# Self-attention in a decoder layer: the transposes of the probabilities stand ahead of the product of probabilities and values in each slot on TensorE

## The chip, the cores and the metric

The kernel runs on one core of one Trainium2 chip, as one program and one launch. The metric is device time in microseconds (us), the median of the runs of a kernel. The engines are named as the profile names them: PE (TensorE, the matrix engine) with PEld for its weight loads, DVE (VectorE), ACT (ScalarE), POOL (GpSimd) and SP (SyncE, which issues most transfers).

## The reference, cut to what matters

One decoder layer: self-attention, cross-attention to a second sequence and a mixture of 16 experts with a shared feed-forward part, each followed by a residual and a layer norm. The change lies in the self-attention, on 32 sequences of 256 tokens with 256 channels, 16 heads and one latent of 72 that serves as keys and as values of every head:

```python
Wdkv = x @ latent_w + latent_b                                  # keys and values, 72 wide
q = jnp.einsum('btc,hcl->bhtl', x, Wd_w) + Wd_b[None, :, None, :]
scores = jnp.einsum('bhtl,bsl->bhts', q, Wdkv) / sqrt(d_head)
scores = jnp.where(causal[None, None, :, :], scores, -jnp.inf)
attn = jax.nn.softmax(scores, axis=-1)
y = jnp.einsum('bhts,bsl->bhtl', attn, Wdkv)
z = jnp.transpose(y, (0, 2, 1, 3)).reshape(b, t, h * Wdkv.shape[-1])
return z @ out_w + out_b
```

## The kernel before

**Numbers in two parts.** Nearly every product is made from operands that are split into a high and a low part (`_hi`, `_lo`). ACT copies a result out of its PSUM bank as the high part; DVE subtracts that from the bank and writes the low part. A bank is free for its next product only when DVE has read it. `three` (lines 128 to 132) then issues three matmuls for one product, `two` (lines 135 to 139) two.

**Slots.** Self-attention is a software pipeline of slots, one for each pair of heads of a sequence, so 256 in all (in the code `g`), and every engine walks through the same list of slots `m` with its own part of the work. In slot m, PE works on five different pairs at once, each at another stage (`SL, IL, TL, PL, OL = 6, 7, 8, 10, 12`): the scores of pair m-6, the transposes of the probabilities of pair m-8, the product of probabilities and values of pair m-10, and the output projection of pair m-12. The probabilities are a triangle of three 128x128 blocks for a head, so a slot has six transposes, three for each of the pair's two heads (`hh`).

**Groups.** 16 slots are a group: two sequences. In the first slot of a group PE projects the latent of the group's two sequences (`KV_MM`), and in the second it transposes that (`KV_TR`) into the keys' and values' other layout. A group has nine tiles of queries to project, in the slots that `Q_SLOT` lists (2, 3, 5, 6, 8, 9, 11, 12, 14). So slots 1, 4, 7, 10, 13 and 15 of a group have no projection on PE; they are called bare slots below. The output projection isn't even either: it has 8 matmuls in most slots, but where four pairs share filled-up rows (`packed`) it has 4, 4, 10 and 10. In the order of PE, the 4s come in slots 0, 1, 8 and 9 of a group, the 10s in slots 2, 3, 10 and 11.

**Banks.** PE has one bank `Q` for projections, two banks `SC` for scores, two banks `TR` for transposes (one for each `hh`), one bank `PV` for the product of probabilities and values, and two banks `O`. In a slot DVE reads the score banks (line 922), makes the reciprocals of the sums (934), writes the low part of the projection if there is one (945), the low part of y from bank `PV` (957) and the two low parts of the transposed probabilities from the banks `TR` (964). ACT copies out the projection (833), then y (844), then the two transposed heads (852), and takes the four exponentials (865). POOL scales the probabilities by the reciprocals (599, 601), a slot ahead of the transposes. Each engine does its instructions strictly in this order.

**What PE waits for.** Before the transposes of head `hh` PE waits for POOL's scaled probabilities (`p_done`) and for DVE to have read the same bank in the slot before (`pTlo_done` of pair g-1). Before the product of probabilities and values it waits for the low parts of its operand, made two slots earlier (`pTlo_done` of pair g), and for DVE to have read bank `PV` in the slot before (`ylo_done` of g-1). ACT waits for that product (`pv_mm`) before it copies y, and y stands ahead of the two transposed heads on ACT and on DVE.

After slot 264 the cross-attention begins; it and the experts follow and are not touched.

Of the kernel before, what the change touches and what calls it, by code (L numbers as in the profile page):

```python
# [33 lines left out]
P = 128  # L34
# [11 lines left out]
RING = 4  # L46
# [17 lines left out]
def need(eng, sem, count):  # L64

    if not isinstance(count, int) or count > 0:
        if isinstance(sem, Later):
            eng.wait_ge(sem.own, sem.base + count)
        else:
            eng.wait_ge(sem, count)  # L70
# [57 lines left out]
def three(pe, out, stat_hi, stat_lo, mov_hi, mov_lo, start, stop):  # L128

    pe.matmul(out, stat_hi, mov_hi, start=start, stop=False, skip_group_check=True)  # L130
    pe.matmul(out, stat_hi, mov_lo, start=False, stop=False, skip_group_check=True)  # L131
    return pe.matmul(out, stat_lo, mov_hi, start=False, stop=stop, skip_group_check=True)  # L132


def two(pe, out, stat_hi, stat_lo, mov_hi, mov_lo, start, stop):

    pe.matmul(out, stat_hi, mov_hi, start=start, stop=False, skip_group_check=True)  # L137
    rows = slice(0, AT + REST)
    return pe.matmul(out, stat_lo[rows], mov_lo[rows], start=False, stop=stop, skip_group_check=True)  # L139
# [48 lines left out]
def upto_slot(J, g, per=1, more=0):  # L188

    return J * (SA_BODY * per) + (per * (g + 1) + more)  # L190


def upto_group(J, c, per=1, more=0):

    return J * (SA_GROUPS * per) + (per * (c + 1) + more)
# [7 lines left out]
def upto_tile(J, t, per=1, more=0):  # L203

    return J * (SA_GROUPS * QT * per) + (per * (t + 1) + more)
# [17 lines left out]
def slot_exists(J, g):  # L223
    return not isinstance(J, int) or 0 <= SA_BODY * J + g < B * NP


def group_exists(J, c):
    return not isinstance(J, int) or 0 <= SA_GROUPS * J + c < GROUPS
# [59 lines left out]
def self_attention(nc, al, bank, ident, cross, d):  # L288
# [28 lines left out]
    prob = al.sb("prob", [P, RING, 2, 3 * P])  # L317
# [9 lines left out]
    Q, SC, TR, PV, O = bank[0], bank[1:3], bank[3:5], bank[5], bank[6:8]  # L327
# [3 lines left out]
    def first_body(J):  # L331
        return isinstance(J, int) and J == 0
# [10 lines left out]
    def kv_bank(J, c):  # L343

        return PV if isinstance(J, int) and SA_GROUPS * J + c == 0 else Q
# [18 lines left out]
    inv_done, p_done = al.sem("inv_done"), al.sem("p_done")  # L364
    p_tr, pThi_done, pTlo_done = al.sem("p_tr"), al.sem("pThi_done"), al.sem("pTlo_done")
# [22 lines left out]
    SL, IL, TL, PL, OL = 6, 7, 8, 10, 12  # L388
# [254 lines left out]
    def tensor(pe):  # L643
# [33 lines left out]
        def slot(J, m):  # L677
            g = m - SL
            if slot_exists(J, g):
                c, p, i = g // GROUP, g % GROUP // 2, g % 2  # L680
                r, k = p % RING, c % 2
# [9 lines left out]
                for hh in range(2):  # L691
                    need(pe, s_read, upto_slot(J, g - 1, 4, 2 * hh - 2))
                    for t in range(TT):
                        tk, keys = slice(t * P, t * P + P), slice(0, (t + 1) * P)
                        mm = two(pe, SC[hh][:, t * T:t * T + (t + 1) * P], q[:, r, hh, 0, i, tk], q[:, r, hh, 1, i, tk],
                                 kvT_a[:, k, i, keys], kvT_b[:, k, i, keys], True, True)
# [4 lines left out]
            elif u == KV_MM and group_exists(J, c):  # L701
                need(pe, xlo_done, upto_row(J, c, 1))
                need(pe, qlo_done, upto_tile(J, c * QT - 1))
                for k in range(KC):
                    mm = three(pe, kv_bank(J, c)[:], lw_hi[:, k], lw_lo[:, k], x_hi[:, c, k], x_lo[:, c, k], k == 0, k == KC - 1)
# [6 lines left out]
            if t is not None and group_exists(J, c):  # L712
                j = t % QT
                w = slice(j * P, j * P + P)
                if first_body(J) and t in SPLIT_BEFORE:
                    pe.wait_ge(w_lo, SPLIT_BEFORE[t])
                if j == 0 and kv_bank(J, c) is Q:
                    need(pe, kv_done, upto_group(J, c))
                elif first_body(J) and t == DIRECT // 2:
                    pe.wait_ge(head_lo, 1)  # L720
                else:
                    need(pe, qlo_done, upto_tile(J, t - 1))
                for k in range(KC):
                    mm = three(pe, Q[:], wd_hi[:, k, w], wd_lo[:, k, w], x_hi[:, c, k], x_lo[:, c, k], k == 0, k == KC - 1)
                mm.then_inc(q_mm, 1)
            g = m - PL
            if slot_exists(J, g):
                r, k, i = g % 2, g // GROUP % 2, g % 2
                if g % GROUP == 0:
# [4 lines left out]
                three(pe, out, kv_hi[:, k, i, 0], kv_lo[:, k, i, 0], pT_hi[:, r, :, 0:T], pT_lo[:, r, :, 0:T], True, False)  # L734
                three(pe, out[:, :, P:T], kv_hi[:, k, i, 1], kv_lo[:, k, i, 1], pT_hi[:, r, :, T:3 * P],
                      pT_lo[:, r, :, T:3 * P], False, True).then_inc(pv_mm, 1)
            g = m - TL
            if slot_exists(J, g):
                r = g % RING
                for hh in range(2):  # L740
                    need(pe, p_done, upto_slot(J, g, 2, hh - 1))
                    need(pe, pTlo_done, upto_slot(J, g - 1, 2, hh - 1))
                    for n in range(3):
                        mm = pe.transpose(TR[hh][:, n * P:n * P + P], prob[:, r, hh, n * P:n * P + P], ident[:])  # L744
                    mm.then_inc(p_tr, 1)
            if u == KV_TR and group_exists(J, c):
                if first_body(J) and c == 0:
                    pe.wait_ge(const, CONST)
# [1 line left out]
                for i in range(2):  # L750
                    for t in range(TT):
                        mm = pe.transpose(kv_bank(J, c)[:, i * T + t * P:i * T + t * P + P], kvT[:, i, t * P:t * P + P], ident[:])
                mm.then_inc(kv_tr, 1)
            g = m - OL
            if slot_exists(J, g):
                r, c, p, i = g % RING, g // GROUP, g % GROUP // 2, g % 2
# [12 lines left out]
                for part, n, a, hh in parts:  # L769
# [4 lines left out]
                    for t in range(TT):  # L774
                        tk = slice(t * P, t * P + P)
                        mm = pe.matmul(O[i][:, t * C:t * C + C], part[rows, n, hh % 2, tk], ow[rows, a, w],
                                       start=p == 0 and a == 0 and hh == 0 and t == 0, stop=p == NP - 1 and a == 1 and hh == 1,
                                       skip_group_check=True)
# [1639 lines left out]
```

## Time and profile before

| | |
|---|---|
| Three runs | 3105.13, 3105.47 (median), 3105.76 us |
| Profiled execution, first to last instruction (span) | 3102.5 us |
| Instructions | 72815 |
| PE, PEld | 3065.7 us (99%), 2875.5 us (93%) |
| DVE, ACT, POOL | 2256.5 us (73%), 2144.2 us (69%), 1587.6 us (51%) |

The page gives no time of its own for the profiled execution but its span, which leaves out what lies before the first and after the last instruction; the median of the runs is 3.0 us above it.

A row of the timeline gives the start in us from the start of the span, the length in us, engine, line, operation, the program's name of what is written and read, and how many instructions were merged into the row. In brackets stands how long the engine had been idle before it and what ended that. A matmul's length contains its way through the array; the next one starts before it ends, so the distance between two starts is what an instruction costs PE. "sa_" is self-attention; "bank" is PSUM.

### The profile page before, as it was taken

What the parts mean: (1) busy time and instruction counts of PE and PEld (TensorE: products, weight loads), DVE (VectorE), ACT (ScalarE), POOL (GpSimd) and SP (SyncE); (2) the same over time, 40 slices, a digit from 0 to 9 for tenths busy, and PEclk for the clock granted to TensorE, in tenths of its full rate; (3) what the DMA queues carried; (4) which work ended last, traced back from release to release, by engine and by line L of the source; (5) the groups of instructions that cost most, each with busy time, mean ns of one, the idle gap of its engine ahead of it and who ended that gap; (6) DMA issues with size and microseconds to landing.
All of it is one profiled execution on the core that took longest, in us unless ns stands there. A gap on an engine that the chain in (4) does not pass through costs nothing. (4 is left out here: it accounts for less than half of the span.)

```text
span 3102.5 us, 72815 instructions
## 1 busy us (share of the span) xinstructions
PE 3065.7 (99%) x22529; PEld 2875.5 (93%) x22529; DVE 2256.5 (73%) x6595; ACT 2144.2 (69%) x6949; POOL 1587.6 (51%) x2918
## 2 busy tenths in 40 slices
PE   9999999999999999999999999999999999999998
PEld 7999999999999999999999999999988888889998
DVE  7888888887787777778878788787765555454665
ACT  8888888888888887788787887887744444442222
POOL 5676677666666665333333333333456666652000
PEclk9999999999999999999999999999999999999999
DMA  5455555544444461111111211111354445533333
GB/s 160 131 158 158 161 156 154 150 128 127 123 118 125 131 214 43 59 46 55 56 46 49 65 46 49 63 45 49 103 139 106 102 107 112 114 53 92 125 122 102
DMA packets 209569, 321.06 MB, mean 103 GB/s; under 512 B 36416, under 2 KB 143040, under 8 KB 208224
## 3 DMA queue, kind: packets, MB, share of 16 engines
q1 hardware_dynamic: 184672, 283.59, 30.4%
q0 software_dynamic: 24576, 33.57, 6.4%
q8 instruction: 154, 2.52, 0.3%
q14 instruction: 167, 1.37, 0.1%
HBM read 125.20 MB, written 75.50 MB: 65 GB/s over the span
## 5 line engine op out<-in xcount | busy, mean ns | idle before, releaser
L1185 POOL TENSOR_SCALAR ca_prob<-ca_prob,ca_inverse 128x120 f32<-128x120 f32 x1024 | 358.4, 369 | 612.6 <-DVE ca_inverse L1484 610.5
L865 ACT ACTIVATE sa_prob<-sa_prob,sa_shift 128x128 f32<-128x128 f32 (+1 forms) x1024 | 453.7, 461 | 0.0
L1425 ACT ACTIVATE ca_prob<-bank,ca_shift 128x120 f32<-128x120 f32 x1024 | 355.0, 368 | 1.8 <-DVE ca_shift L1478 0.5
L922 DVE CUSTOM_DVE_ANT_0 sa_prob<-bank,sa_mask 128x128 f32<-128x128 f32 (+1 forms) x1024 | 303.5, 351 | 6.1 <-issue 5.3
L599 POOL TENSOR_SCALAR sa_prob<-sa_prob,sa_inverse 128x128 f32<-128x128 f32 x512 | 198.1, 387 | 208.8 <-DVE sa_inverse L934 197.6
L139 PE MATMUL bank<-sa_kvT_b,sa_q 112*128 112x128 f32 (+1 forms) x1024 | 260.2, 279 | 0.0
L964 DVE TENSOR_TENSOR sa_pT_lo<-bank,sa_pT_hi 128x384 fp32r<-128x384 f32 x512 | 258.2, 544 | 0.2 <-ACT sa_pT_hi L852 0.2
L601 POOL TENSOR_SCALAR sa_prob<-sa_prob,sa_inverse 128x256 f32<-128x256 f32 x512 | 252.3, 493 | 0.0
L137 PE MATMUL bank<-sa_kvT_a,sa_q 128*128 128x128 f32 (+1 forms) x1024 | 249.3, 280 | 1.2 <-DVE sa_shift L922 0.9
L1917 POOL DMA_INDIRECT mid_acc<-ex_out,ex_to_tokens x112 | 190.6, 1702 | 97.7 <-DVE ex_out L2229 68.8
L852 ACT ACTIVATE sa_pT_hi<-bank 128x384 fp32r<-128x384 f32 x512 | 222.9, 493 | 0.5 <-PE bank L744 0.5
L957 DVE TENSOR_TENSOR sa_y_lo<-bank,sa_y_hi 96x512 fp32r<-96x512 f32 (+1 forms) x256 | 175.0, 684 | 63.3 <-ACT sa_y_hi L844 62.2
L1425 ACT ACTIVATION_READ_ACCUMULATOR ca_prob<-bank,ca_shift 128x1 f32 x1024 | 220.1, 215 | 0.0
L2107 ACT ACTIVATE ex_act_g<-bank 128x512 f32<-128x512 f32 x128 | 76.4, 597 | 203.1 <-PE bank L132 192.2
L744 PE MATMUL bank<-all_ident,sa_prob 128*128 128x128 f32 x1536 | 210.6, 273 | 1.4 <-POOL sa_prob L601 1.4
L844 ACT ACTIVATE sa_y_hi<-bank 128x512 fp32r<-128x512 f32 x256 | 153.1, 598 | 84.3 <-PE bank L132 82.4
L865 ACT ACTIVATION_READ_ACCUMULATOR sa_prob<-sa_prob,sa_shift 128x1 f32 x1024 | 210.4, 205 | 0.0
L1385 ACT ACTIVATE ca_q_hi<-bank 128x256 fp32r<-128x256 f32 x256 | 99.0, 387 | 158.2 <-PE bank L132 152.0
L945 DVE SCALAR_TENSOR_TENSOR sa_q_tile<-bank,sa_qbias,sa_q_tile 128x512 fp32r<-128x512 f32 x141 | 105.8, 750 | 127.5 <-ACT sa_q_tile L833 126.8
L2194 DVE TENSOR_TENSOR ex_hid<-ex_act_g,bank 128x512 f32<-128x512 f32 x128 | 87.4, 687 | 152.4 <-PE bank L132 149.9
L137 PEld LDWEIGHTS bank<-sa_kvT_a,sa_q 128*128 128x128 f32 x1024 | 195.5, 191 | 2.5 <-DVE sa_shift L922 1.3
L139 PEld LDWEIGHTS bank<-sa_kvT_b,sa_q 112*128 112x128 f32 x1024 | 195.5, 191 | 0.0
(274 smaller groups left out, 11915.3 us busy)
## 6 DMA issues: line engine op xcount, KB each, us to landing
sa_q<-sa_q_tile SPq DMA_DIRECT2D x125, 288.0 KB
sa_q<-sa_q_tile SPq DMA_DIRECT2D x157, 112.0 KB
mid_x2T<-ca_x2T SPq DMA_DIRECT2D x32, 512.0 KB, 3.0
ex_sx<-mid_x2T SPq DMA_DIRECT2D x32, 512.0 KB
sa_q<-sa_q_tile SPq DMA_DIRECT2D x297, 32.0 KB
sa_xT_raw<-in_xT SPq DMA_DIRECT2D x32, 256.0 KB, 2.9
sa_q<-sa_q_tile SPq DMA_DIRECT2D x32, 256.0 KB
sa_x_res<-in_x SPq DMA_DIRECT2D x32, 256.0 KB
```

Of the source, the lines that this page charges most:

```text
L137: pe.matmul(out, stat_hi, mov_hi, start=start, stop=False, skip_group_check=True)
L139: return pe.matmul(out, stat_lo[rows], mov_lo[rows], start=False, stop=stop, skip_group_check=True)
L599: pool.tensor_scalar(prob[:, r, hh, 0:P], prob[:, r, hh, 0:P], inverse[:, r, 2 * hh:2 * hh + 1], 1.0, ALU.mult, ALU.mult)
L601: pool.tensor_scalar(prob[:, r, hh, P:3 * P], prob[:, r, hh, P:3 * P], inverse[:, r, 2 * hh + 1:2 * hh + 2], 1.0, ALU.mult, ALU.mult).then ...
L744: mm = pe.transpose(TR[hh][:, n * P:n * P + P], prob[:, r, hh, n * P:n * P + P], ident[:])
L852: act.activation(pT_hi[:, r, hh], TR[hh][:, 0:3 * P], ACT.Copy).then_inc(pThi_done, 1)
L865: act.activation(prob[:, r, hh, cols], prob[:, r, hh, cols], ACT.Exp, bias=shift[:, r, n:n + 1], scale=-1.0, accum_out=total[:, r, n:n + 1 ...
L922: dve.tensor_tensor_reduce(out=prob[:, r, hh, cols], in0=SC[hh][:, t * T:t * T + (t + 1) * P], in1=mask[:].rearrange("p a s -> p (a s)")[: ...
L964: dve.tensor_tensor(pT_lo[:, r, hh], TR[hh][:, 0:3 * P], f32(pT_hi[:, r, hh]), ALU.subtract).then_inc(pTlo_done, 1)
L1185: ins = pool.tensor_scalar(prob[:, r, t, hh], prob[:, r, t, hh], inverse[:, r, n:n + 1], 1.0, ALU.mult, ALU.mult)
L1425: act.activation(prob[:, r, t, hh], SC[g % 2][:, n * S:n * S + S], ACT.Exp, bias=shift[:, r, n:n + 1], accum_out=total[:, r, n:n + 1]).the ...
L1917: pool.indirect_dma_start(d["acc"].rearrange("b t c -> (b t) c"), bass.IndirectOffsetOnAxis(ap=of[:, j:j + 1], axis=0), out[:, i, t], None ...
```

## The change

The block that issues the six transposes is moved ahead of the block that issues the product of probabilities and values. Nothing else is changed: no instruction is added or removed, each block keeps its waits, and the other four queues have the same rows in the same order.

```diff
@@ tensor(pe), slot(J, m), behind the projection of the queries
+            g = m - TL
+            if slot_exists(J, g):
+                r = g % RING
+                for hh in range(2):
+                    need(pe, p_done, upto_slot(J, g, 2, hh - 1))
+                    need(pe, pTlo_done, upto_slot(J, g - 1, 2, hh - 1))
+                    for n in range(3):
+                        mm = pe.transpose(TR[hh][:, n * P:n * P + P], prob[:, r, hh, n * P:n * P + P], ident[:])
+                    mm.then_inc(p_tr, 1)
             g = m - PL
             if slot_exists(J, g):
                 r, k, i = g % 2, g // GROUP % 2, g % 2
...
                 three(pe, out[:, :, P:T], kv_hi[:, k, i, 1], kv_lo[:, k, i, 1], pT_hi[:, r, :, T:3 * P],
                       pT_lo[:, r, :, T:3 * P], False, True).then_inc(pv_mm, 1)
-            g = m - TL
-            if slot_exists(J, g):
-                r = g % RING
-                for hh in range(2):
-                    need(pe, p_done, upto_slot(J, g, 2, hh - 1))
-                    need(pe, pTlo_done, upto_slot(J, g - 1, 2, hh - 1))
-                    for n in range(3):
-                        mm = pe.transpose(TR[hh][:, n * P:n * P + P], prob[:, r, hh, n * P:n * P + P], ident[:])
-                    mm.then_inc(p_tr, 1)
```

On PE, in a bare slot in the steady part of the pipeline, this stood before. L137 and L139 end the scores, L130 to L132 are the product of probabilities and values, L744 the transposes:

```order
L137 MATMUL bank<-sa_kvT_a,sa_q 128x256
L139 MATMUL bank<-sa_kvT_b,sa_q 128x256
L130 MATMUL bank<-sa_pT_hi,sa_kv_hi 128x512 [waits sa_ylo_done,sa_pTlo_done,sa_kv_done]
L131 MATMUL bank<-sa_pT_lo,sa_kv_hi 128x512
L132 MATMUL bank<-sa_pT_hi,sa_kv_lo 128x512
L130 MATMUL bank<-sa_pT_hi,sa_kv_hi 128x2x128
L131 MATMUL bank<-sa_pT_lo,sa_kv_hi 128x2x128
L132 MATMUL bank<-sa_pT_hi,sa_kv_lo 128x2x128
L744 MATMUL bank<-all_ident,sa_prob 128x128 [waits sa_pTlo_done,sa_p_done]
L744 MATMUL bank<-all_ident,sa_prob 128x128 x2
```

And this stands there now; the transposes have become L733:

```order
L137 MATMUL bank<-sa_kvT_a,sa_q 128x256
L139 MATMUL bank<-sa_kvT_b,sa_q 128x256
L733 MATMUL bank<-all_ident,sa_prob 128x128 [waits sa_pTlo_done,sa_p_done]
L733 MATMUL bank<-all_ident,sa_prob 128x128 x2
L733 MATMUL bank<-all_ident,sa_prob 128x128 [waits sa_pTlo_done,sa_p_done]
L733 MATMUL bank<-all_ident,sa_prob 128x128 x2
L130 MATMUL bank<-sa_pT_hi,sa_kv_hi 128x512 [waits sa_ylo_done,sa_pTlo_done,sa_kv_done]
L131 MATMUL bank<-sa_pT_lo,sa_kv_hi 128x512
L132 MATMUL bank<-sa_pT_hi,sa_kv_lo 128x512
L130 MATMUL bank<-sa_pT_hi,sa_kv_hi 128x2x128
```

The six transposes with their two waits now follow the scores directly, and the product follows them.

Between one slot's product and the next slot's scores, on PE, this stood before (L776 is the output projection):

```order
L131 MATMUL bank<-sa_pT_lo,sa_kv_hi 128x2x128
L132 MATMUL bank<-sa_pT_hi,sa_kv_lo 128x2x128
L744 MATMUL bank<-all_ident,sa_prob 128x128 [waits sa_pTlo_done,sa_p_done]
L744 MATMUL bank<-all_ident,sa_prob 128x128 x2
L744 MATMUL bank<-all_ident,sa_prob 128x128 [waits sa_pTlo_done,sa_p_done]
L744 MATMUL bank<-all_ident,sa_prob 128x128 x2
L776 MATMUL bank<-sa_ow,sa_y_hi 128x256 [waits sa_ydup_done,sa_ylo_done]
L776 MATMUL bank<-sa_ow,sa_y_hi 128x256 x3
```

And now:

```order
L131 MATMUL bank<-sa_pT_lo,sa_kv_hi 128x2x128
L132 MATMUL bank<-sa_pT_hi,sa_kv_lo 128x2x128
L776 MATMUL bank<-sa_ow,sa_y_hi 128x256 [waits sa_ydup_done,sa_ylo_done]
L776 MATMUL bank<-sa_ow,sa_y_hi 128x256 x3
```

What moved there: the transposes no longer lie between the product and the output projection.

## Rows read from the trace of the kernel before

**Rows 1.** The page: busy time, share of the span and instructions of each engine.

```profile
PE 3065.7 (99%) x22529; PEld 2875.5 (93%) x22529; DVE 2256.5 (73%) x6595; ACT 2144.2 (69%) x6949; POOL 1587.6 (51%) x2918
```

**Rows 2.** Busy time by stretch: self-attention's steady part; three short ones (PEclk: granted clock).

```profile
34.00:38.00 4.00, 3.12 (x15) 2.66 (x15) 3.64 (x15) 3.81 (x12) 2.42 (x6) 0.66 0.14 32
...
65.00:68.00 3.00, 1.52 (x14) 1.35 (x13) 2.39 (x5) 3.00 (x12) 2.68 (x5) 1.00 0.83 266
...
40.00:1165.00 1125.00, 1114.73 (x7901) 1036.07 (x7900) 906.99 (x3387) 924.03 (x2997) 771.14 (x1468) 1.00 0.51 145
```

**Rows 3.** What PE waited for, whole span: us in total, times, longest.

```profile
PE bank L130 <- DVE sa_kv_lo L968: 8.8, 15, 1.5
PE bank L130 <- DVE sa_y_lo L957: 2.2, 3, 1.0
```

**Rows 4.** Timeline, all engines, slot 12 of a group and the bare slot 13.

```profile
762.28 0.82 PE L744 MATMUL bank<-all_ident,sa_prob 128*128 128x128 f32 x6
762.48 0.60 ACT L844 ACTIVATE sa_y_hi<-bank 128x512 fp32r<-128x512 f32 x1 [0.36 <-PE bank L132]
762.85 0.71 PE L776 MATMUL bank<-sa_ow,sa_y_hi 128*128 128x256 f32 x4
...
763.11 0.69 DVE L957 TENSOR_TENSOR sa_y_lo<-bank,sa_y_hi 96x512 fp32r<-96x512 f32 x1 [0.21 <-ACT sa_y_hi L844]
...
763.72 1.01 DVE L964 TENSOR_TENSOR sa_pT_lo<-bank,sa_pT_hi 128x384 fp32r<-128x384 f32 x2
763.88 0.22 PE L137 MATMUL bank<-sa_kvT_a,sa_q 128*128 128x128 f32 x1
...
764.81 0.40 PE L130 MATMUL bank<-sa_pT_hi,sa_kv_hi 128*128 128x512 f32 x1
...
765.86 0.82 PE L744 MATMUL bank<-all_ident,sa_prob 128*128 128x128 f32 x6
```

**Rows 5.** The page: the low part of the transposed probabilities, one head.

```profile
L964 DVE TENSOR_TENSOR sa_pT_lo<-bank,sa_pT_hi 128x384 fp32r<-128x384 f32 x512 | 258.2, 544 | 0.2 <-ACT sa_pT_hi L852 0.2
```

**Rows 6.** Timeline of start-up: transposes that wait for POOL, with their weight load.

```profile
25.45 0.49 POOL L601 TENSOR_SCALAR sa_prob<-sa_prob,sa_inverse 128x256 f32<-128x256 f32 x1
...
25.99 0.31 PEld L744 LDWEIGHTS bank<-all_ident,sa_prob 128*128 128x128 f32 x3 [0.49 <-POOL sa_prob L601]
...
25.99 0.55 PE L744 MATMUL bank<-all_ident,sa_prob 128*128 128x128 f32 x3 [0.26 <-POOL sa_prob L601]
26.29 0.31 PE L137 MATMUL bank<-sa_kvT_a,sa_q 128*128 128x128 f32 x1
```

**Rows 7.** Timeline, slots 9 and 10 of the same group: PE and POOL.

```profile
748.73 0.82 PE L744 MATMUL bank<-all_ident,sa_prob 128*128 128x128 f32 x6
...
749.86 0.22 PE L137 MATMUL bank<-sa_kvT_a,sa_q 128*128 128x128 f32 x1
...
750.63 0.48 POOL L601 TENSOR_SCALAR sa_prob<-sa_prob,sa_inverse 128x256 f32<-128x256 f32 x1
```

**Rows 8.** Timeline, slots 0 to 2 of a group, up to the first query projection.

```profile
707.73 0.82 PE L744 MATMUL bank<-all_ident,sa_prob 128*128 128x128 f32 x6
...
709.07 0.68 DVE L957 TENSOR_TENSOR sa_y_lo<-bank,sa_y_hi 72x512 fp32r<-72x512 f32 x1
...
711.02 0.82 PE L744 MATMUL bank<-all_ident,sa_prob 128*128 128x128 f32 x6
...
712.59 0.22 PE L137 MATMUL bank<-sa_kvT_a,sa_q 128*128 128x128 f32 x1
...
713.39 0.68 DVE L968 TENSOR_TENSOR sa_kv_lo<-bank,sa_kv_hi 128x512 fp32r<-128x512 f32 x1
...
714.12 0.50 PE L130 MATMUL bank<-sa_xT_hi,sa_wd_hi 128*128 128x512 f32 x1 [0.45 <-DVE sa_kv_lo L968]
```

**Rows 9.** Timeline of PE, the last two slots that have transposes.

```profile
1156.58 0.82 PE L744 MATMUL bank<-all_ident,sa_prob 128*128 128x128 f32 x6
...
1159.58 0.82 PE L744 MATMUL bank<-all_ident,sa_prob 128*128 128x128 f32 x6
```

## The prediction

> **What bounds the kernel now.** I read the page's busy times first: PE is busy 99% of the span, and no other engine more than 73% [rows 1]. Then the same by stretch: in the 1125 us of self-attention's steady part PE is busy 1114.73 us at a granted clock of 1.00, DVE 906.99 and ACT 924.03 [rows 2]. So PE's queue sets the time there, and it has nothing to gain from better cover: the list of PE's waits has 8.8 us on the low part of the keys and values, in 15 waits (one for each group from the second on), and 2.2 us on the low part of y [rows 3]. Every new wait on PE is paid in full. Last I read the timeline of one slot on all engines, to see how late the evictions are for their next use. The reader is to see there that they hang on one event: the end of the product of probabilities and values.
>
> **The clock of one slot.** Let t be the time at which PE has issued that product and goes on; in slot 12 it is 762.28, where the transposes start now. ACT starts the copy of y at t+0.20, having idled for it. DVE starts the low part of y at t+0.83, having idled for that copy; then come the two low parts of the transposed probabilities, merged in one row, from t+1.44 to t+2.45 [rows 4]. One of them takes 0.54 us [rows 5], so the first bank of transposes is free at t+1.98 and the second at t+2.45. These times hang on t and not on the transposes, since y stands first on both engines and its copy is longer than the transposes of the first head. With the new order the transposes are already done at t, and the chain behind t stays as long as it is.
>
> PE meanwhile: six transposes 0.57 us (762.28 to 762.85), an output projection with 8 matmuls 1.03 (762.85 to 763.88), the scores 0.93 (to 764.81), the product 1.05 (to 765.86) [rows 4]. With 4 matmuls the output projection takes 0.56 (748.73 to 749.86 is 1.13, less 0.57 for the transposes) [rows 7]; with 10, I take 8 matmuls' 1.03 and two more at its mean of 0.13, 1.29, an estimate from rows 4.
>
> **What the move does.** It adds and removes no instruction, so no PE work is priced. It changes who is late for whom.
>
> Before, PE came back to the transposes after output projection, scores and product, counted from its own last transpose: t + 0.57 + 1.03 + 0.93 + 1.05 = t+3.58 in slot 13, against banks free at t+2.45. The slack was 1.1 us, with 4 matmuls 0.65 us. Now the product no longer lies in between. PE comes at t + 1.03 + 0.93 = t+1.96 (8 matmuls), t+1.49 (4) or t+2.22 (10), in a bare slot. Where a projection of queries stands in the slot, its six matmuls of 512 columns add 1.40 us (an estimate from the product, whose 2304 columns take 1.05), PE comes at t+2.89 or later, and there is no wait.
>
> The price of a wait itself I take from start-up, where transposes wait for POOL: the releaser ended at 25.45 + 0.49 = 25.94, the first of three transposes started at 25.99, and the next work at 26.29 [rows 6]. So 0.05 from release to start and 0.30 for three transposes. In a bare slot the second head's transposes therefore start at t+2.45+0.05 and PE is through them at t+2.80. Unhindered it would be at t+1.96+0.57 = 2.53, 2.06 or 2.79. The stall is 0.27 us with 8 matmuls ahead, 0.74 with 4 and 0.01 with 10. The output projection that counts is that of the slot before:
> - slot 4 (10 matmuls): 0.01
> - slots 7, 13 and 15 (8): 3 x 0.27 = 0.81
> - slot 10 (4): 0.74.
>
> One page has a rule on this. The Trainium skill, TensorE: Matmul & The Clock Gate, section "Architectural detail: the array is 16× 32×32, not 1× 128×128", says that PE's queue can pull weight loads ahead of matmuls in flight. Here the weight is the block of probabilities, and its load starts at 25.99 with the transpose, not ahead of the wait [rows 6]; by the rule alone, with the load done in advance, each waited-for half would be a few hundredths of a us shorter and the sum perhaps 3 us less. The measurement decides, and the 0.30 holds.
>
> **Slots 0 to 2.** Before, slot 0's product ended at 707.73; now six transposes come first, and t(0) = 708.30. DVE began y's low part at 709.07 and would now begin at t+0.83 = 709.13: the chain hangs on t again. PE is through slot 1's transposes at 708.30+2.80 = 711.10 and t(1) = 712.15. Before, t(1) was 711.02, and slot 2's first projection started at 714.12, after a wait of 0.45 for the low part of keys and values, which DVE had begun at t(1)+2.37 behind both transposes [rows 8]. That wait hangs on t(1) too: the projection now starts at 712.15 + 3.10 = 715.25, which is 1.13 us later. The existing wait grows from 0.45 to about 1, because PE comes 0.57 us sooner, and 0.57 us is the stall in slot 1. So a group costs 0.01 + 0.81 + 0.74 + 1.13 = 2.7 us, and 15 groups (the count of the waits in rows 3) 40.5 us.
>
> **Start and end.** The first group has one bare slot in the steady order (15) and start-up slots whose chain I can't lay out; I take 1.5 us, bounded by 0 and by 4 (the sum of the waits there would have to double). Behind the last group there are six slots with scores and without a projection (0.27, 0.74, 0.74, 0.01, 0.01, 0.27), of which two come after the layer norm's statistics on DVE, for which I add 0.4 each by estimate (0 to 1.0), and two slots without scores: the transposes stand 1156.58 and 1159.58, 3.00 us apart [rows 9], and would stand t+2.80+1.05 = 3.85 apart, 0.85 more each. Together 2.04 + 0.8 + 1.7 = 4.5 us.
>
> **The sum.** 40.5 + 1.5 + 4.5 = 46.5 us on a span of 3102.5, so 3149 us of span; the median of the runs is 3.0 above the span, 3105.47, and so I forecast 3105.47 + 46.5 = 3152 us, 1.5% slower. Nothing behind takes it back: the cross-attention hangs on PE's end of self-attention, and rows 3 show no wait there of more than about a us.
>
> POOL's probabilities are the other wait of the moved block, 1.05 us nearer now. The tightest bare slot I found is 10: POOL ends at 750.63+0.48 = 751.11 and may slip by the 0.57 that t slips, to 751.68; PE's second half waits for DVE until 748.73+0.57+2.50 = 751.80 [rows 7]. It is hidden by 0.1 us. If POOL slipped in other slots by 0.5 us beyond that, it would cost 15 us more, and I keep this for the upper end. For the lower end: if the two output projections with 4 matmuls and slots 0 to 2 stall as reckoned but the three 0.27s vanish (they rest on a slack of a quarter of a us), a group costs 1.9 and the sum is 34 us; if also the keys' wait does not grow, 1.3 us and 25.
>
> **Rivals.**
> - *Not slower.* PE finds the banks free, because DVE would take the transposed probabilities sooner than t+1.44: they are ready at t, and the end of each bare slot decides, t+1.49 to t+2.22. For it speaks that the transposes come earlier. Against it: y's copy and y's low part stand ahead in both queues, and DVE idled 0.21 us for y in rows 4, so only a DVE that passes both by t+1.4 would do it. Then the one effect is the other way: bank PV gets 0.57 us more until its next use, the 2.2 us of waits on y vanish [rows 3], and the time is 3103.3. 4%. With partial cover it stays within 0.2%: 6%.
> - *The clock falls in the stalls.* Between 34 and 38 the granted clock was 0.66 where PE was busy 3.12 of 4 us, but it was 1.00 between 65 and 68 with 1.52 of 3 us busy [rows 2]. So gaps can cost clock, and a single gap of over 1 us need not. If each of the two larger stalls of a group cost what the stretch at 34 did, (1-0.66) x 4 = 1.4 us, that is 15 x 2 x 1.4 = 42 us on top: 3194. 5%. The Trainium skill, Perfetto Trace Analysis, section "Matmul Optimizations", says that the matmul engine scales with utilization and wants its matmuls back to back; by it this rival would be likelier, by rows 2 it is not.
> - *The loop feeds on itself.* A stalled PE delays scores and so DVE's reading of them and POOL, and bare slots cost 0.5 us more each for POOL: 3152 + 15 = 3167 to 3175. 12%.
> - *The forecast*, its own range 3138 to 3166: 73%.
>
> About 0.2% (6 us) is what a measurement of this kernel can tell from no change. By the cases: faster by more 3%, within 7%, slower 90%. The range, with both bounds of start and end and the partial cases, is 3128 to 3174.
>
> **What would show it.** In the profile after, PE's waits list a new line, transposes waiting for DVE's low part of the transposed probabilities, some 100 times, a few tenths each, about 25 to 35 us in all; the line on the keys' low part grows from 8.8 to 15 to 18 us; the line on y is gone. The steady stretch is longer by about 45 us, all other stretches by nothing, at a clock of 1.00. In slot 7, 10, 13 and 15 the distance from t to the end of the transposes is 2.8 us whatever lies between. The forecast is wrong if the transposes wait for POOL instead, if the pair of low parts starts before t+1.3, or if the stretch's length is unchanged.

## The result and the profile after

The changed kernel takes 3167.4 us (median of 5 runs, 3166.2 to 3168.0), the kernel before 3105.4 beside it: 1.0202 times as long, with an interval of 1.0191 to 1.0213, so 62 us slower. The forecast was 3152 us, 46.5 us slower, its range 3128 to 3174. The direction and the mechanism held; the sum was a quarter too small.

The page of the kernel after first, in the columns of [rows 1]:

```profile
PE 3095.8 (98%) x22529; PEld 2869.2 (91%) x22529; DVE 2249.7 (71%) x6595; ACT 2143.1 (68%) x6949; POOL 1575.8 (50%) x2918
```

DVE, ACT and POOL did the same work within some 12 us. PE's own row grew by 30 us, though it issues the same 22529 matmuls. A transpose's row is 0.27 us long where the next one starts 0.11 us behind it, so when PE stalls, the last row covers the first part of the stall and counts as busy. The span is the measure.

The stretch of self-attention's steady part, as in [rows 2] (length, PE, PEld, DVE, ACT, POOL, granted clock):

```profile
40.00:1225.00 1185.00, 1142.09 (x7898) 1026.72 (x7897) 898.75 (x3387) 925.71 (x3001) 763.78 (x1469) 1.00 0.48 138
```

The same 7900 matmuls that fitted into 1125 us now fill 1185, at a granted clock of 1.00. So in the steady part the rival with the falling clock is out. PE's waits over the span, against [rows 3]:

```profile
PE bank L733 <- DVE sa_pT_lo L964: 18.2, 31, 1.0
PE bank L130 <- DVE sa_kv_lo L968: 16.6, 15, 1.2
PE bank L733 <- POOL sa_prob L601: 6.2, 11, 1.6
PE bank L130 <- DVE sa_y_lo L957: 1.6, 2, 1.0
```

The two lines that were forecast are there, and the one on the keys' low part grew from 8.8 to 16.6 us. The new one has only 31 entries, as a stall of a few tenths lies mostly under the row before it, and it is in the distances that one must read those.

The bare slot 13 on all engines, against [rows 4]. The end of the last product, t, is 800.80, where the output projection starts:

```profile
800.80 0.64 PE L776 MATMUL bank<-sa_ow,sa_y_hi 128*128 128x256 f32 x4
801.01 0.60 ACT L844 ACTIVATE sa_y_hi<-bank 128x512 fp32r<-128x512 f32 x1 [1.01 <-PE bank L132]
801.64 0.69 DVE L957 TENSOR_TENSOR sa_y_lo<-bank,sa_y_hi 96x512 fp32r<-96x512 f32 x1 [0.86 <-ACT sa_y_hi L844]
801.75 0.23 PE L137 MATMUL bank<-sa_kvT_a,sa_q 128*128 128x128 f32 x1
802.25 1.00 DVE L964 TENSOR_TENSOR sa_pT_lo<-bank,sa_pT_hi 128x384 fp32r<-128x384 f32 x2
...
802.93 0.98 PE L733 MATMUL bank<-all_ident,sa_prob 128*128 128x128 f32 x6
803.67 0.48 PE L130 MATMUL bank<-sa_pT_hi,sa_kv_hi 128*128 128x512 f32 x1
803.99 0.39 PE L131 MATMUL bank<-sa_pT_lo,sa_kv_hi 128*128 128x512 f32 x1
...
804.81 0.40 PE L776 MATMUL bank<-sa_ow,sa_y_hi 128*128 128x256 f32 x2
```

DVE starts y at t+0.84 and the two low parts at t+1.45, as before to 0.01. The six transposes begin at t+2.13 and last until 803.67, 0.74 us where they took 0.57: the second three waited inside the row. The first three waited too, by some 0.25 us: PE was through the scores 0.93 after their start at 801.75, at t+1.88, and the first bank came free at t+1.99. That costs nothing of its own, as the second bank comes later. From t to the next product's end it is 4.01 us. That number is the mark of the change. Measured from one product's end to the next, in the slots 0 to 15 of one group in the middle:

| slot | 0 | 1 | 2 | 3 | 4 | 5 | 6 | 7 | 8 | 9 | 10 | 11 | 12 | 13 | 14 | 15 |
|---|---|---|---|---|---|---|---|---|---|---|---|---|---|---|---|---|
| before | 4.98 | 3.27 | 5.66 | 5.21 | 3.82 | 4.98 | 4.98 | 3.59 | 4.97 | 4.50 | 3.10 | 5.22 | 5.22 | 3.58 | 4.98 | 3.58 |
| after | 4.98 | 4.00 | 6.32 | 5.21 | 4.01 | 4.98 | 4.99 | 4.01 | 4.98 | 4.49 | 4.00 | 5.22 | 5.23 | 4.01 | 4.98 | 4.00 |

Every slot with a projection of queries behind the second is unchanged to 0.02 us. Every bare slot takes 4.0 us, whether its own work is 3.1, 3.6 or 3.8: it is as long as the chain that hangs on t (y's copy, y's low part, the two low parts of the transposed probabilities, then PE's last transposes and the product), not as the work. Slot 2 is 0.66 longer. The last place is the wait for the keys and values, against [rows 8]; t(1) is 747.42:

```profile
747.42 0.60 PE L752 MATMUL bank<-all_ident,sa_kvT 128*128 128x128 f32 x4
...
748.86 1.01 DVE L964 TENSOR_TENSOR sa_pT_lo<-bank,sa_pT_hi 128x384 fp32r<-128x384 f32 x2
749.78 0.68 DVE L968 TENSOR_TENSOR sa_kv_lo<-bank,sa_kv_hi 128x512 fp32r<-128x512 f32 x1
...
750.52 0.50 PE L130 MATMUL bank<-sa_xT_hi,sa_wd_hi 128*128 128x512 f32 x1 [1.10 <-DVE sa_kv_lo L968]
```

DVE is at the keys' low part at t(1)+2.36 and PE at its projection at t(1)+3.10, as before to 0.01; PE was there earlier, and so waited 1.10 us instead of 0.45.

### The profile page after: what moved, and what is told of

Its sections match the earlier page's. It is cut to its first block and busy times, and to the rows that moved or that the text cites. A ratio compares the mean times of both kernels' runs of the same rounds, so it can differ in the third digit from the quotient of the medians.

```text
span 3164.7 us, 72815 instructions
## 1 busy us (share of the span) xinstructions
PE 3095.8 (98%) x22529; PEld 2869.2 (91%) x22529; DVE 2249.7 (71%) x6595; ACT 2143.1 (68%) x6949; POOL 1575.8 (50%) x2918
## 5 line engine op out<-in xcount | busy, mean ns | idle before, releaser
L957 DVE TENSOR_TENSOR sa_y_lo<-bank,sa_y_hi 96x512 fp32r<-96x512 f32 (+1 forms) x256 | 175.2, 684 | 194.5 <-ACT sa_y_hi L844 192.8
L844 ACT ACTIVATE sa_y_hi<-bank 128x512 fp32r<-128x512 f32 x256 | 153.4, 599 | 224.3 <-PE bank L132 224.1
L139 PE MATMUL bank<-sa_kvT_b,sa_q 112*128 112x128 f32 (+1 forms) x1024 | 260.6, 280 | 0.0
L964 DVE TENSOR_TENSOR sa_pT_lo<-bank,sa_pT_hi 128x384 fp32r<-128x384 f32 x512 | 258.1, 543 | 0.2 <-ACT sa_pT_hi L852 0.2
L733 PE MATMUL bank<-all_ident,sa_prob 128*128 128x128 f32 x1536 | 227.2, 277 | 28.5 <-DVE sa_pT_lo L964 18.2
L137 PE MATMUL bank<-sa_kvT_a,sa_q 128*128 128x128 f32 (+1 forms) x1024 | 249.8, 280 | 1.1 <-DVE sa_shift L922 0.9
L733 PEld LDWEIGHTS bank<-all_ident,sa_prob 128*128 128x128 f32 x1536 | 173.8, 140 | 81.0 <-POOL sa_prob L601 33.2
L852 ACT ACTIVATE sa_pT_hi<-bank 128x384 fp32r<-128x384 f32 x512 | 222.4, 492 | 0.5 <-PE bank L733 0.5
L137 PEld LDWEIGHTS bank<-sa_kvT_a,sa_q 128*128 128x128 f32 x1024 | 196.6, 192 | 2.2 <-DVE sa_shift L922 1.3
L130 PE MATMUL bank<-sa_pT_hi,sa_kv_hi 128*128 128x512 f32 (+1 forms) x512 | 196.2, 383 | 1.6 <-DVE sa_y_lo L957 1.6
L139 PEld LDWEIGHTS bank<-sa_kvT_b,sa_q 112*128 112x128 f32 x1024 | 196.6, 192 | 0.0
```

Source lines behind the costliest of these rows:

```text
L964: dve.tensor_tensor(pT_lo[:, r, hh], TR[hh][:, 0:3 * P], f32(pT_hi[:, r, hh]), ALU.subtract).then_inc(pTlo_done, 1)
```

## The experiments

Theory A is the forecast's: y and the transposed probabilities are evicted in a chain behind the product's end, and PE comes back to the transposes' banks before it is through. Rival B: transposes ahead of the product cost PE something of its own. Rival C: PE waits for POOL's probabilities. Medians are to be read beside 3104 for the kernel before, measured with them (3104.1 to 3104.3).

**e1: transposes ahead in slots with a projection only** (condensed: `transposes()` and `product()` stand for the two blocks).

```diff
-            transposes(); product()          # always
+            if (t is not None or u == KV_MM) and group_exists(J, c):
+                transposes(); product()
+            else:
+                product(); transposes()
```

> The transposes stand ahead of the product only in the slots in which PE also projects (nine with queries, and slot 0 of a group), and behind it in the bare slots. Theory A (in a bare slot PE now comes back to the transposes' banks before DVE, whose reads hang on the end of the last product, has left them; the changed kernel's 4.01 us per bare slot is that chain): the chain is covered by the product in bare slots and by the projection in the others, so nearly all of the 62 us is gone: 3105 to 3111 us, the rest being the product that now waits about 0.1 to 0.2 us for y in the slots behind 4 output matmuls. Rival B (each block of transposes ahead of the product costs PE something of its own, whatever DVE does, by weight loads or by the way the instructions follow each other): 10 of 16 slots keep their cost, 3105 + 39 = 3144. Rival C (PE waits for POOL's probabilities): POOL is tightest in bare slots, so about 3105 to 3115 too.

3121.5 us, ratio 1.0052 (1.0035 to 1.0068), +17 and not +39: B is out as stated, since ten of sixteen slots have the new order and the stalls are gone. But A's 1 to 7 us were too few. The distances show where: most pairs of slots add up to what they did (4.99 + 2.93 + 5.64 for slots 6 to 8, 13.54 before), but slots 10 and 11 together take 8.68 instead of 8.32, and slots 0 to 2 take 15.02 instead of 13.91, of which 0.65 is handed over from the slot before by the shorter bare slot 15. A bare slot behind 4 output matmuls now takes 2.79, where its work is 2.5: its product waits for y of the slot before, in the other bank, whose low part ends at t+1.52 by the same chain. In slot 2 the wait for keys and values grows too:

```profile
PE bank L130 <- DVE sa_kv_lo L976: 11.6, 15, 1.6
```

**e2: transposes ahead in bare slots only**, the two branches of e1 exchanged.

> The complement: the transposes stand ahead of the product only in the bare slots (1, 4, 7, 10, 13, 15 of a group and the slots at the end). Theory A: what counts is the way from the end of the last product to the transposes. The slot before a bare one now has its own transposes in that way again (0.57 us), so of the stalls only a rest of 0.2 to 0.3 us is left in slots 1 and 10, and the product of slot 1 ends 0.57 us later, which the wait for the low part of keys and values hands on in full: 0.8 + 0.3 = 1.1 us for a group, 16 us, and about 5 in the bare slots at the end: 3120 to 3130 us. So A expects e1 and e2 together to cost much less than 62. Rival B: the two add up, 6 of 16 slots, 3105 + 23 = 3128. Rival C: all of the cost, about 3160.

3134.1 us, 1.0093 (1.0077 to 1.0110), +30; A had 16 to 26, so it missed by 4. By its total alone it does not tell A from B (3128). The timeline does. This is bare slot 13, which took 4.01 in the changed kernel:

```profile
704.50 0.82 PE L734 MATMUL bank<-all_ident,sa_prob 128*128 128x128 f32 x6
...
706.10 0.22 PE L137 MATMUL bank<-sa_kvT_a,sa_q 128*128 128x128 f32 x1
...
707.04 0.82 PE L734 MATMUL bank<-all_ident,sa_prob 128*128 128x128 f32 x6
707.61 0.48 PE L130 MATMUL bank<-sa_pT_hi,sa_kv_hi 128*128 128x512 f32 x1
```

The transposes follow the scores without a gap and take their plain 0.57 us, in the very order that stalled before, because the last slot's transposes lie once more between t and them. It is the way from t that counts, not the order. What is left is in slots 1, 2 and 10 and at the end. One group lost 2 us in slots 10 to 13 for another reason: ACT's copy of the projection started at 250.34 after 1.98 us of waiting for a transfer of queries. e1 and e2 cost 47 us together, so the parts are not as unlike the sum as I expected ("much less than 62"); each brings a small wait of its own.

**e3: only the first head's transposes ahead** (condensed).

```diff
-            transposes((0, 1)); product()
+            transposes((0,)); product(); transposes((1,))
```

> Only the three transposes of the first head stand ahead of the product, those of the second behind it. Theory A: the first bank is free at about t+2.1 (t is the end of the product), PE comes at t+1.78 behind 4 output matmuls (0.3 us late), t+2.25 behind 8 and t+2.5 behind 10 (no stall); the second bank is not waited for any more. With 0.3 for the keys' wait: about 1.1 us for a group, 3105 + 16 + 3 = 3124 us (3118 to 3130). Rival B: half of the transposes ahead, half of 62: 3136. Rival C: POOL's first head is ready 0.8 us before its second, about 3110.

3123.8 us, 1.0061 (1.0044 to 1.0077): A's 3124. As it says, there is a stall behind 4 output matmuls (slot 10: 3.55 instead of 3.10) and none behind 8 or 10 (3.59 and 3.84 in slots 7 and 4).

**e4: POOL scales half of the columns** (the rest stays unscaled; condensed).

```diff
-  prob[:, r, hh, 0:P]      prob[:, r, hh, P:3 * P]
+  prob[:, r, hh, 0:P // 2] prob[:, r, hh, P:2 * P]
```

> The changed kernel, with POOL scaling 64 of 128 and 128 of 256 columns of each head's probabilities (the other half is left unscaled, so the result is not the reference's); POOL is done with a pair some 0.5 us earlier. Theory A: POOL is hidden nearly everywhere, 3162 to 3168 us (the start, the end and three groups in which slot 10 took 4.3 us instead of 4.0 can give back a little). Rival B: the same. Rival C (PE waits for the probabilities in bare slots): six bare slots of a group give 0.3 to 0.5 us each, 3120 to 3140.

3166.1 us. C is out. POOL got faster by less than the 0.5 us expected: in slot 10 its second head ends at t+2.06 and not t+2.39. But every bare slot is as long as it was, and the 1 us between the medians is no more than the kernel before differed by (3104.3 here, 3105.4 beside the result). The list of waits puts 6.2 us down to POOL in the kernel after and still 7.0 us in this one, with half of the columns; where two releasers end close together, the list's choice between them means little.

**e5: y's low part, half of the columns** (the rest keeps old values).

```diff
+  cols = slice(0, 2 * T if SA_BODY * J + g < GROUP else T)
-  dve.tensor_tensor(y_lo[...], PV[low, :], y_hi[...], ALU.subtract)
+  dve.tensor_tensor(y_lo[...][:, cols], PV[low, cols], y_hi[...][:, cols], ALU.subtract)
```

> The changed kernel, with DVE writing only half of the columns of y's low part from slot 16 on (the other half keeps old values, so the result is not the reference's). y's low part stands ahead of the transposed probabilities on DVE, and should take about 0.27 us less. Theory A: every stalled bare slot gets shorter by just that, 4.01 to 3.74, where it does not meet PE's own work first (3.84 with 10 output matmuls), and the wait for keys and values too: 5 x 0.27 + 0.17 + 0.27 = 1.8 us for a group, 27 us, and 1.6 at the end: 3167.4 - 28 = 3139 us (3134 to 3144). Rival B: no change, 3167. Rival C: no change or a few us, 3163 to 3167.

3145.7 us, 1.0136 (1.0120 to 1.0153), 22 us off the changed kernel, of the 28 expected. y's row went from 0.69 to 0.42 us, and the bare slots from 4.01 to 3.79: 0.22 of the 0.27 expected. Slot 4, whose work is 3.83, stopped there. Slot 10 stopped at 3.89: POOL's second head ends at t+2.39 there, now behind DVE's second low part at t+2.23, and PE waits for POOL. In the other bare slots an instruction that PE never waits for by name sets part of their length.

**e6: the transposed probabilities ahead of y** on ACT and DVE (the blocks L852 and L964 stand before L844 and L957).

> The changed kernel, with the transposed probabilities ahead of y on ACT and on DVE. The two buffers of transposed probabilities stay, so ACT still waits for the last product before it writes them. Theory A: the second transposes' bank is free at about t+1.75 instead of t+2.45, in time; now bank PV is late: y's low part ends at about t+2.5, and the product starts at about t+2.62 and takes 1.14: bare slots of about 3.75 us instead of 4.01, 3.84 with 10 output matmuls. 1.66 us for a group less, 25 us: 3140 us (3134 to 3148). Rival B: no change, 3167. Rival C: no change.

3143.0 us, 1.0129 (1.0112 to 1.0146): A's 3140 within its range. The bare slots took 3.67 us (expected 3.75), but for slot 4, bound by its work of 3.83, and slot 10, which took 3.94 and waits for POOL as in e5: now bank PV is the one that comes late. A shuffle of the evictions moves the stall from one bank to the other.

**e7: the same with three buffers** for the transposed probabilities (condensed; the unscaled probabilities get three instead of four).

```diff
-    pT_hi, pT_lo = al.split("pT", [P, 2, 2, 3 * P])        prob = [P, RING, 2, 3 * P]
+    pT_hi, pT_lo = al.split("pT", [P, 3, 2, 3 * P])        prob = [P, 3, 2, 3 * P]
-                        need(act, pv_mm, upto_slot(J, g - 2))
+                        need(act, pv_mm, upto_slot(J, g - 3))
```

> As e6, and with three buffers of transposed probabilities instead of two (the unscaled probabilities get three instead of four, to make room), so that ACT need not wait for the product of the same slot: the transposed probabilities are read while the product runs. Theory A: no bank is late any more; bare slots are as long as PE's own work, 3.10, 3.58 or 3.84 us; the wait for keys and values shrinks below that of the kernel before, as DVE has less ahead of it: 3098 to 3105 us, all of the 62 us back and a little more. Rival B: the order on PE still costs what it costs: 3160 or more. Rival C: POOL is as late as before: 3160 or more.

3105.0 us, 1.0003 (0.9993 to 1.0013). All 62 us are back with the transposes still ahead of the product. Some 5 of them are a gain that the kernel before does not have: the wait for the keys' low part is 4.2 us here and 8.8 there. So the total alone leaves room for a few us of the order's own; the bare slots leave little. One of them, t = 690.83:

```profile
690.71 1.01 DVE L957 TENSOR_TENSOR sa_pT_lo<-bank,sa_pT_hi 128x384 fp32r<-128x384 f32 x2
...
690.83 0.63 PE L776 MATMUL bank<-sa_ow,sa_y_hi 128*128 128x256 f32 x4
...
691.66 0.69 DVE L964 TENSOR_TENSOR sa_y_lo<-bank,sa_y_hi 96x512 fp32r<-96x512 f32 x1
...
692.71 0.82 PE L733 MATMUL bank<-all_ident,sa_prob 128*128 128x128 f32 x6
```

(In this kernel L957 is the transposed probabilities.) DVE starts them 0.12 us before t, no longer 1.45 after it, and bare slots are 3.12, 3.60 and 3.84 again, within 0.03 of before. It was not faster than before, though a little more was in the expected range: slot 2 is 5.38 instead of 5.66, but slot 1 is 3.34 instead of 3.27 and the bare slots have their hundredths more, so that the 14 groups from the first full one to the last gain only 1.3 us, and start and end took that.

**e8: the kernel before, with keys and values evicted first** in slot 1 (blocks L856 and L968 ahead of L852 and L964).

> The kernel before (product ahead of the transposes), with the keys and values of slot 1 of each group copied and split ahead of the transposed probabilities on ACT and DVE. The wait of 8.8 us for the low part of keys and values is the largest of the kernel before. Theory A (PE waits there for a chain behind the end of the product, which is long only because of what stands ahead in DVE's queue): that wait vanishes, and since weights are loaded in time again 0.1 us more for each: 3105.4 - 8 to 10 = 3096 us (3094 to 3099). Rival: DVE's reads of the transposes, now later, delay slot 2's transposes or the scores by as much: 3105.

3096.3 us, 0.9976 (0.9966 to 0.9986): 8 us faster than the kernel before, as expected. t(1) is 633.57 here:

```profile
634.40 0.69 DVE L957 TENSOR_TENSOR sa_y_lo<-bank,sa_y_hi 72x512 fp32r<-72x512 f32 x1
635.49 0.69 DVE L961 TENSOR_TENSOR sa_kv_lo<-bank,sa_kv_hi 128x512 fp32r<-128x512 f32 x1 [0.41 <-ACT sa_kv_hi L848]
...
636.24 0.50 PE L130 MATMUL bank<-sa_xT_hi,sa_wd_hi 128*128 128x512 f32 x1
```

The low part of the keys comes at t(1)+1.92 instead of +2.37, PE starts the projection at t(1)+2.67 instead of +3.10, and the line of 8.8 us in PE's waits is down to 0.2.

**e9: the changed kernel with e8's edit.**

> The changed kernel (transposes ahead of the product), with the keys and values of slot 1 copied and split ahead of the transposed probabilities on ACT and DVE, as in e8. Theory A: in the changed kernel the wait for the low part of keys and values is 16.6 us in 15 waits, because it hangs on the end of slot 1's product, which the move delays, while PE comes sooner. With this edit the low part is ready 0.9 us sooner after that product (one pair of low parts less ahead of it); PE still waits 0.2 to 0.3. Slots 1 to 2: 6.32 to about 5.4 us, 15 times, so 3167.4 - 14 = 3153 us (3150 to 3156). The six bare slots keep their 4.01. If the growth of that wait were no term of its own but only the stall of slot 1 seen again, nothing would be gained beyond the 8 us that e8 gained: 3159.

3152.4 us, 1.0155 (1.0140 to 1.0171): 15 us off the changed kernel, A's 3153. Slot 2 fell from 6.32 to 5.38, the bare slots stayed at 4.0. The edit is worth nearly twice what it is worth in the kernel before (15 and 8 us). The difference, 7 us, is what the growth of this wait has in the 62; against e8, where the wait is gone too, the move still costs 56 us (3152.4 and 3096.3).

**e10: e8, and in slot 0 DVE splits the latent (L950) behind the transposed probabilities.**

> e8 (product ahead of the transposes, keys and values first), and in slot 0 DVE splits the new latent behind the transposed probabilities instead of ahead of y's low part. In e8 slot 1 takes 3.27 us where its work is 3.10: its product waits for y's low part of slot 0, which stands behind the latent on DVE. Theory A: that wait vanishes, 0.16 us in most of 15 groups: 3096.3 - 2.4 = 3094 us (3092 to 3096), faster than both kernels. Rival: POOL gets the latent later (it makes the second copy from it) and is late with slot 2's probabilities: 3096 or more.

3095.7 us, 0.9973 (0.9964 to 0.9982), runs from 3093.6 to 3099.1. It is faster than both kernels, but 0.6 us against e8 is inside the scatter. In the traces the wait is gone: slot 1 takes 3.11 us in all 15 groups, where in e8 it took 3.27 or more in 13, and the 14 groups from the first full one to the last are 1.5 us shorter in all. Whether the whole kernel keeps that is open.

## Why the prediction was right, and where it was short

- **The chain behind t** (y's copy at t+0.20, y's low part at +0.83, the transposed probabilities from +1.44 to +2.45, all hanging on t and not on the transposes): right, to 0.01 us, and shown by e5 and e6, which change the chain and with it the slots, and by e7, which unhooks the transposed probabilities from it.
- **Which slots stall**: right. Bare slots do, those with a projection do not, but for the handed-on wait in slot 2. That the bare slot with 10 output matmuls ahead would stall by only 0.01 was too low: 0.19.
- **The price of a wait**: this is the term that was mis-sized. The prediction took 0.05 from release to start and 0.30 for the second three transposes, from start-up waits on POOL, and 1.05 for the product, and so 3.85 us from t to t. Measured 4.01. Of the 0.16, 0.07 is the release: on PE the second low part ended at 802.25 + 1.00 = 803.25 and the product began at 803.67, 0.42 later and not 0.35. The other 0.09 belongs to the transposes. They follow each other at 0.11 us, so six take 0.65, but the row behind them is drawn from 0.03 us after the last one's start and is 0.09 longer (the product's first matmul has 0.48 and is followed after 0.32, 803.67 to 803.99; the others have 0.39 and 0.23). The 0.57 that the prediction read from [rows 4] left that 0.09 out. Before, it stood in the output projection behind the transposes (1.03 there, 0.95 now, 800.80 to 801.75), and now it stands in the product (1.14, where [rows 4] have 1.05). In a slot that PE's own work bounds, the 0.09 only changes its place; in a slot that the chain bounds, it stands behind the chain and is added. 0.16 us in six bare slots and 0.09 in slot 2 are 1.05 us for a group.
- **Slots 0 to 2**: 1.13 forecast, 0.73 + 0.66 = 1.39 measured; the handing-on itself was right (t(1)+3.10 to the digit), the rest is the 0.16 and 0.09 above.
- **The sum**: a group cost 3.62 us on the mean and not 2.7. The latent's transposes in slot 1 stand at 64.50 and 1070.01 before and at 68.17 and 1124.31 after, so 54.30 - 3.67 = 50.6 us in 14 groups. Of the 3.67 at the start 0.90 belongs to slot 1 of the first full group (4.01 instead of 3.11), 2.8 are left against 1.5 forecast. What lies behind the last full group cost about 5 us, 4.5 forecast. How much of the 2.8 the move made is open, as the granted clock fell there, and not alike in all executions. In the kernel after it was 0.73 between 30 and 40 us (0.50, the 1.2 GHz level, from 36 to 40, behind four us of which PE was busy 2.2) and 0.93 in the ten us behind; in the kernel before it was 0.83 and 1.00; in e5, whose edit begins only in slot 26, it stayed at 1.00, and the latent's transposes of the first full group come at 65.83 instead of 68.17. Kernel after, then e5, in the columns of [rows 2]:

```profile
30.00:40.00 10.00, 7.92 (x35) 6.49 (x34) 7.69 (x27) 7.84 (x25) 5.60 (x12) 0.73 0.36 90
...
30.00:40.00 10.00, 7.12 (x47) 5.72 (x46) 8.03 (x28) 8.62 (x27) 5.99 (x14) 1.00 0.36 90
```

- **POOL hidden by 0.1 us in slot 10**: right. POOL's second head ends at t+2.39 and DVE's second low part at t+2.45; e4 moved POOL by 0.33 us and no bare slot changed. In two of the 15 groups slot 10 took 4.3 us instead of 4.0, 0.6 us in all (the expectation of e4 says three), and so it did in e4, where POOL ends at t+2.06 in them. What is late is ACT, which has one more copy (L879, an operand of the cross-attention) ahead of the projection's and y's. So y's copy starts at t+0.32 and DVE's two low parts at t+1.73 instead of t+1.44 (the changed kernel, t = 182.60):

```profile
181.83 0.63 ACT L879 ACTIVATE early_st_hi<-early_st_raw 128x512 fp32r<-128x512 f32 x1
...
184.33 1.01 DVE L964 TENSOR_TENSOR sa_pT_lo<-bank,sa_pT_hi 128x384 fp32r<-128x384 f32 x2
```

- **The rival "the loop feeds on itself"**: 3167.4 lies in its span (3167 to 3175) and 1.4 us above the forecast's own (3138 to 3166), so by the number alone the rival would have won. Its mechanism, POOL late in the bare slots, is what e4 excludes. It is luck that the measured time still lies below 3174: that room was kept for POOL, and the 0.16 us in each bare slot used it. The rival was also priced too low in its own terms: 0.5 us in six bare slots of 15 groups are 45 us and not 15.
- **The clock rival**, which by the Trainium skill (Perfetto Trace Analysis, section "Matmul Optimizations") was likelier: it did not come true in the steady part. Bare slots are up to 0.9 us longer than their work there, and the granted clock stayed at 1.00, the 2.4 GHz level. It fell at the start alone, as above, before the move and after it.
- **What the profile would show**: "some 100 times, 25 to 35 us" for the transposes' wait was wrong as a forecast of the list, which had 18.2 in 31, because short stalls aren't in it. The keys' line grew to 16.6, as forecast; the line on y is not gone but went from 2.2 to 1.6 us; the steady stretch is 60 us longer and not 45; t to the end of the transposes is 2.87 and not 2.8.

## What to carry to other kernels

A step that is moved in a full queue changes every distance between the freeing of a buffer and its next use, even if no work is added; take the event on which the evictions hang and count from it the time until each bank's next writer, slot by slot, at the leanest slot. If slots with different work come out equally long, as here, look for a chain that sets them; its members can be shortened, reordered or given another buffer to find out. Before reordering the bound engine, look at the engines that serve it: here the order of two evictions in one slot of sixteen was worth 8 us, and the order on TensorE cost 62.

## What the runs showed of the hardware that was not expected

Transposes of 128 columns follow each other at 0.11 us. The first matmul behind such a block is drawn 0.03 us after the last transpose's start and is followed after 0.32 us, where 0.23 is usual for 512 columns. That is so whether there was a wait (803.67 to 803.99, slot 13) or not (slot 12):

```profile
799.66 0.48 PE L130 MATMUL bank<-sa_pT_hi,sa_kv_hi 128*128 128x512 f32 x1
...
799.98 0.40 PE L131 MATMUL bank<-sa_pT_lo,sa_kv_hi 128*128 128x512 f32 x1
```

After a release by DVE the weight load came 0.12 us behind the end of the releasing row (803.25 to 803.37), after one by POOL 0.05: in start-up (25.94 to 25.99, [rows 6]), and in slot 10 of e5, where POOL's row ends at 699.35 + 0.48 = 699.83 and the load starts at 699.88. Why the two differ is not shown. Kernel after, then e5:

```profile
803.37 0.31 PEld L733 LDWEIGHTS bank<-all_ident,sa_prob 128*128 128x128 f32 x3 [0.15 <-issue]
...
699.35 0.48 POOL L601 TENSOR_SCALAR sa_prob<-sa_prob,sa_inverse 128x256 f32<-128x256 f32 x1
...
699.88 0.31 PEld L733 LDWEIGHTS bank<-all_ident,sa_prob 128*128 128x128 f32 x3 [0.24 <-POOL sa_prob L601]
```
